# Writing the even pairs' score banks from VectorE in each image's last attention block

## The reference

```
h = group_norm1(x, n2_g, n2_b)
N = H * W
q = conv1x1(h, q_w, q_b).reshape(B, C, N).transpose(0, 2, 1)
k = conv1x1(h, k_w, k_b).reshape(B, C, N)
v = conv1x1(h, v_w, v_b).reshape(B, C, N).transpose(0, 2, 1)
scale = C ** (-0.5)
attn = jax.nn.softmax(jnp.einsum('bnc,bcm->bnm', q, k) * scale, axis=-1)
out = jnp.einsum('bnm,bmc->bnc', attn, v)
return x + out
```

## Time and profile before

| | us |
|---|---|
| median of 3 runs | 2844.68 (2842.29 to 2845.42) |
| profiled execution, its own time | 2840.18 |
| profiled execution, its span | 2838.4 |

### The profile page before, as it was taken

One profiled execution on the slowest core, in us unless ns is written; L12 is line 12 of the kernel. 1 busy time (PEld: TensorE's weight loads), 2 busy tenths in 40 slices (PEclk: granted clock), 3 DMA queues, 4 the chain that ended last, 5 costly groups with the idle time before them and its releaser, 6 DMA issues.

```text
span 2838.4 us, 54486 instructions
## 1 busy us (share of the span) xinstructions
PE 2763.5 (97%) x19644; PEld 933.7 (33%) x19644; DVE 2519.0 (89%) x3182; ACT 2223.6 (78%) x2321; POOL 1826.2 (64%) x1479
## 2 busy tenths in 40 slices
PE   7889999999999999999988999999999999999998
PEld 4233333333333333333323333333333333333332
DVE  5689999999999999999768999999999999999984
ACT  4467888888888888888866788888888888888887
POOL 1446666666666666666664666666666666666666
PEclk9999999999999999999999999999999999999999
DMA  6103000000000000000000000000000000000000
GB/s 203 40 9 75 10 11 10 11 10 10 11 10 11 11 10 11 10 11 9 5 5 16 9 10 11 10 11 10 11 10 11 11 10 11 11 10 11 9 5 5
DMA packets 35768, 48.20 MB, mean 17 GB/s; under 512 B 7848, under 2 KB 33960, under 8 KB 34992
## 3 DMA queue, kind: packets, MB, share of 16 engines
q1 hardware_dynamic: 35504, 44.75, 6.0%
HBM read 16.41 MB, written 9.44 MB: 9 GB/s over the span
## 4 chain that ended last, share of the span: by engine, by line
PE 88%; DVE 8%; issue 3%; ACT 1%; POOL 0%; DMA 0%; POOLq 0%; DVEq 0%; SPq 0%; ACTq 0%
PE ps L950 39%; PE ps L941 33%; PE ps L957 11%; DVE mxp L759 4%; PE ps L1058 2%; DVE arena L782 1%; DVE ps L772 1%; PE ps L973 1%; ACT arena L532 0%; DVE ps L775 0%; PE ps L1085 0%; PE ps L1034 0%; PE ps L1142 0%; PE ps L1100 0%; PE ps L966 0%
## 5 line engine op out<-in xcount | busy, mean ns | idle before, releaser
L462 POOL TENSOR_TENSOR arena<-arena 128x512 f32<-128x512 f32 x1224 | 1559.6, 1274 | 798.0 <-ACT arena L532 719.1
L759 DVE TENSOR_REDUCE mxp<-ps 128x1 f32<-128x1024 f32 x1296 | 1575.3, 1219 | 169.0 <-PE ps L957 137.8
L532 ACT ACTIVATE arena<-ps,bnd 128x1024 f32<-128x1024 f32 x1296 | 1374.0, 1111 | 412.8 <-PE ps L941 368.7
L950 PE MATMUL ps<-arena,vals 128*64 128x512 f32 x5184 | 1268.2, 605 | 1.0 <-ACT pvb L542 1.0
L941 PE MATMUL ps<-arena 64*128 64x512 f16 x7776 | 1054.9, 377 | 4.7 <-ACT ps L569 2.9
L775 DVE TENSOR_TENSOR ps<-ps,arena 128x512 f32<-128x512 f32 x1260 | 869.0, 690 | 72.1 <-ACT arena L532 71.2
L569 ACT ACTIVATE ps<-mseed 128x1024 f32<-128x1024 f32 x612 | 629.2, 1028 | 53.3 <-ACT arena L532 0.4
L957 PE MATMUL ps<-arena,QM 64*128 64x512 f16 x2592 | 500.9, 383 | 17.8 <-DVE mxp L759 11.0
L941 PEld LDWEIGHTS ps<-arena 64*128 64x128 f16 x7776 | 375.2, 94 | 423.4 <-issue 31.0
L950 PEld LDWEIGHTS ps<-arena,vals 128*64 128x64 f32 x5184 | 310.8, 136 | 505.4 <-issue 349.1
L957 PEld LDWEIGHTS ps<-arena,QM 64*128 64x128 f16 x2592 | 124.7, 93 | 734.9 <-DVE mxp L759 633.3
(11 more groups left out here) (111 smaller groups left out, 674.4 us busy)
## 6 DMA issues: line engine op xcount, KB each, us to landing
arena<-arena SPq DMA_DIRECT2D x144, 64.0 KB, 2.0
arena<-in_x_rows SPq DMA_DIRECT2D x8, 816.0 KB, 10.0
xs<-in_x SPq DMA_DIRECT2D x4, 1152.0 KB, 16.3
f_scratch<-arena SPq DMA_DIRECT2D x32, 144.0 KB
f<-f_scratch SPq DMA_DIRECT2D x16, 288.0 KB, 9.7
QM<-arena SPq DMA_DIRECT2D x72, 64.0 KB, 2.0
xst<-arena SPq DMA_DIRECT2D x72, 64.0 KB, 1.9
out<-ot SPq DMA_DIRECT2D x72, 64.0 KB, 2.0
```

The costliest lines, as they stand in the source:

```text
L462: nc.gpsimd.tensor_tensor(accA[:, n % 2, :], accA[:, n % 2, :], e, ALU.add).then_inc(adda_free, 1)
L532: nc.scalar.activation(flat(E[:, slot_of(n % 2, p), :, :]), flat(ps[:, S_BANK + 2 * buf:S_BANK + 2 * buf + 2, :]), ACT.Exp, scale=bnd[:, 6 ...
L759: nc.vector.reduce_max(flat(mxp[:])[:, v:v + 1], flat(ps[:, bank:bank + 2, :]), AX.X).then_inc(mx_free, 1)
L950: a = nc.tensor.matmul(ps[C * t:C * t + C, ACC_BANK, :], V[:, p, t, :], E[:, slot_of(par, p), t, :], start=(p == 0), stop=(p == NPAIR - 1) ...
```

## The change

In the last block of an image (`j == NBLK - 1`) VectorE writes `mseed` over the banks of the even pairs 4 to 34, except pair 10, whose bank 0 is used in between for the row sums of the block before: 15 pairs per image, 30 in all. The scores of these pairs leave out their fourth term (two matmuls) and wait for the new semaphore `dve_filled`.

```diff
+        def dve_fills(j, p):
+            return j == NBLK - 1 and 4 <= p < NPAIR and p % 2 == 0 and p != ROW_SUMS + 4
+
+        FILLS = sum(dve_fills(NBLK - 1, p) for p in range(NPAIR))
...
+            def fill(b, j, p):
+
+                n = blk(b, j)
+                dve.wait_ge(mseed_ready, n + 1)
+                dve.wait_ge(e_ready, NPAIR * n + p)
+                nc.vector.tensor_copy(ps[:, S_BANK:S_BANK + 2, :], mseed[:, n % 2, :].unsqueeze(1).to_broadcast([P, 2, CH])
+                                      ).then_inc(dve_filled, 1)
...
@@ def attend(b, j) on VectorE, inside the loop over p @@
+                    if dve_fills(j, p + 2):
+                        fill(b, j, p + 2)
                     if p + 1 < NPAIR:
                         add_b(n, p + 1)
...
-            def scores(par, p, peers, seeds=None):
+            def scores(par, p, peers, seeds=None, fills=None):
...
-                if seeds is not None:
-                    pe.wait_ge(seeded, seeds)
+                if seeds is not None or fills is not None:
+                    if seeds is not None:
+                        pe.wait_ge(seeded, seeds)
+                    else:
+                        pe.wait_ge(dve_filled, fills)
                     terms = terms[:3]
...
-                                             start=(k == 0 and seeds is None), stop=(k == len(terms) - 1),
+                                             start=(k == 0 and seeds is None and fills is None), stop=(k == len(terms) - 1),
...
-                        scores(par, p + 2, n0 + p + 1)
+                        fills = FILLS * b + sum(dve_fills(j, q) for q in range(p + 3)) if dve_fills(j, p + 2) else None
+                        scores(par, p + 2, n0 + p + 1, fills=fills)
```

More of the change, by code:

```diff
@@ L223, in program @@
         seeded = sem("seeded")
+        dve_filled = sem("dve_filled")
         s_ready = sem("s_ready")
```

## The result

The kernel with the change takes 2861.52 us (median of 4 runs, 2859.27 to 2863.14), the kernel before 2844.84 (4 runs): slower, ratio 1.0061, 95% interval 1.0049 to 1.0074. The forecast was 2860.8. The profiled execution took 2859.27 us, with a span of 2857.5, so it is 19.1 us above the profiled execution before; the medians are 16.7 us apart. The profiled execution before was itself a quick one, 4.5 us under its kernel's median; where the rest of the difference lies is told further down.

What follows compares the result with a forecast made beforehand. TensorE bounds the last block, ScalarE close behind; a chain through VectorE makes turns 3.93 us against 3.54, or 4.23 with a reciprocal. That adds 8.04 us per image, 16.1 in all: 2844.68 + 16.1 = 2860.8 us, range 2854 to 2867.

Steps and rivals of the forecast that it cites:

- Signal to TensorE: Chain link in an image's last block: end of VectorE's instruction to the waiting matmul, 0.07 us.
- ScalarE's 0.16: High end for the signal link: from ScalarE's seed end to the waiting matmul, 0.16 us.
- The reciprocal: Stands between add and copy in eight turns per image: 0.30 us more, a turn of 4.23 us.
- +0.75: Last block, pair 2 to 4: 3.18 us now, 3.93 with the change.
- +0.47: Last block, pairs 4 to 8, two turns: 7.39 us now, 7.86 with the change.
- -0.22: Last block, pair 8 to 10: no copy, TensorE bounds it with one fourth term less, 0.22 us saved.
- +0.45: Last block, pair 10 to 12: 3.48 us now, 3.93 with the change.
- +5.49: Last block, pairs 12 to 28, eight turns with a reciprocal: 28.35 us now, 33.84 with the change.
- +1.10: Last block, pairs 28 to 34, three turns: 10.69 us now, 11.79 with the change.
- rival 2: Last blocks: copy hidden in the 1.42 us slack, 6.6 us saved, 2838.1 us; chance 4%.
- Double rate for the copy: Rival 1, VectorE's copy in last blocks: 0.82 us for 1024 columns, +3.8 us, 2848.5 us; chance 7%.
- A lower clock: Rival 3, last blocks: TensorE's clock halves in the chain's gaps, +96 us, some 2940 us; chance 1%.

Runs made afterwards that it cites:

- run 1: Changed kernel with VectorE's copy for pair p + 2 placed ahead of its add of pair p, and so ahead of the reciprocal: 2841.24 us, ratio 0.9993.
- run 2: Changed kernel with the last block's eight reciprocals moved behind the odd pair's add, none between add and copy: 2858.43 us, ratio 1.0048.
- run 5: Changed kernel with copies of 512 columns instead of 1024 (bank 0 only), bank 1's tile keeping its fourth term: 2851.56 us, ratio 1.0028.
- run 3: Changed kernel with copies made and waited for, but the even pairs' scores keep their fourth term and start=True: 2868.88 us, ratio 1.0089.
- run 8: Kernel before, last blocks' odd seeds from pair 5 cut in two (ScalarE bank 2, VectorE bank 3), no copies for even pairs: 2841.63 us, ratio 0.9991.
- run 7: Run 1 plus last blocks' odd seeds from pair 5 cut in two (ScalarE bank 2, VectorE bank 3): 2840.99 us, ratio 0.9989.
- run 4: Changed kernel without copies or their waits, 30 scores with three terms, output not the reference's: 2839.97 us, ratio 0.9988.
- run 6: Changed kernel with the even pairs' copies made by ScalarE behind its even exponentials instead of by VectorE: 2867.26 us, ratio 1.0082.
- run 9: Run 8 with run 4's edit: odd seeds cut in two, three terms in 30 scores, no copies, output not the reference's: 2836.32 us, ratio 0.9974.
- run 10: Run 7 with VectorE's copies only for every second even pair, the others keeping four terms: 2841.04 us, ratio 0.9992.

## Why the prediction was right

**The mechanism.** The forecast was the chain exponentials, add, copy, six matmuls, with both TensorE and ScalarE waiting for it. The chain in the trace is that one, link by link, and four runs take its links apart: without the add and the reciprocal ahead of the copy the loss is gone (run 1), without the reciprocal it falls by 0.25 us a turn (run 2), with a copy 0.53 shorter and scores 0.22 longer it falls by 0.31 (run 5), with two more matmuls it grows by 0.22 (run 3).

**The links.** Exponentials to add: 1.15 forecast, 1.15 measured. Add to copy 0.61 and 0.61. Copy 1.23 and 1.21 to 1.22. Signal to TensorE 0.07 and 0.14: the row chosen was the wrong one. The prediction's other figure, ScalarE's 0.16, is nearer but was no signal either: the odd pair's matmuls at 1417.33 come 0.22 after the two ahead of them, as they do without any wait. Where they do wait for the seed, it is 0.14 (shown below). Six matmuls 0.87 and 0.86. Sum 3.93 and 3.98. The reciprocal 0.30 and 0.25, so the turn with one was met (4.23 and 4.23) by two errors of opposite sign.

**The sum.** Per image, in the prediction's order, forecast and measured: +0.75 and +0.80; +0.47 and +0.57; -0.22 and -0.12; +0.45 and +0.50; +5.49 and +5.48; +1.10 and +1.25. Together +8.04 and +8.48, so 17.0 us for both images where 16.1 were forecast and the medians show 16.7. The -0.12 is pair 8 to 10: the exponentials come 0.86 us after the scores' start at pair 8 (six matmuls) but 1.08 at pair 10 (eight), which takes back the 0.22 of the term, and what is left is the 0.1 us for which the odd pair no longer waits for its seed. The mechanism was right; that the forecast of 2860.8 came within 0.7 us of the median is in part luck, since the links were 0.9 us too short in all and single executions of the kernel before lie up to 3 or 4 us from their median.

**What was imprecise.** "TensorE bounds the block, and ScalarE comes close behind" was not quite so. The prediction saw the wait for the seed, but put it into the turn that it showed, where there is none. It stands in every other turn, as in these rows of both engines, before:

```profile
1419.75 1.03 ACT L569 ACTIVATE ps<-mseed 128x1024 f32<-128x1024 f32 x1
...
1420.60 0.38 PE L941 MATMUL ps<-arena,one 64*128 64x512 f16 x2
...
1420.92 0.82 PE L941 MATMUL ps<-arena 64*128 64x512 f16 x6
```

The seed ends at 1420.78, and the matmuls start 0.14 later, 0.32 after the two ahead of them instead of 0.22. So what ran at 3.54 us was a loop over two turns and both engines: exponentials to the end of the seed and its signal 3.38, scores of the odd pair 0.75, weighing 1.87, scores of the even pair 1.08, together 7.08 (the recorded expectations have 3.40 and 7.10). All turns are down to TensorE's own 3.48 only when the seed comes earlier (run 8). For the forecast it made no difference, as its chain is longer than both. But the price of rival 2, 6.6 us for a hidden copy, was too high: the loop contains the even pair's scores once in two turns, so the removed terms bring half. Measured are 3.9 us for the terms alone (3.0 by the turns of its trace) and 2.7 us with the copy first (run 1, median against median, an interval that includes no change).

**The rivals.** Double rate for the copy: 30 copies took 1206 to 1220 ns, single rate, as the 512-column row had said. The Trainium skill, "VectorE: DVE Perf Modes", has it in another section, "Why PSUM operands drop a tier": an operand in PSUM caps a float32 instruction at single rate. The trace agrees, also for an instruction whose output alone lies there. A hidden copy: its condition, add and copy and signal in 1.42 us, did not hold; they took 2.0. The order of run 1, without the add ahead, needs 1.48 and so comes close. No run made the copy so short or so early that it was hidden with room to spare. A lower clock: it did not come, the granted clock was 1.00 in every 5 us window of both last blocks from pair 2 on.

**What the forecast did not see.** The profiled execution after is 2.1 us longer than two blocks explain. From the first image's end (ScalarE's copy of the weighed values) to ScalarE's first use of the second image's maxima it is 79.88 us before and 81.53 after, although the instructions there are the same: 1.65 of the 2.1 us. The last section has what is known of it.

**A version that beats both.** Run 7, 2840.99 us against 2843.79, is 0.1% faster than the kernel before, with an interval that just excludes 1; run 1 is the smallest edit that undoes the loss. Nothing tells the two apart. With the chain through the copy at 3.45 and TensorE's own work at 3.27, about 0.18 us a turn remain that no run which keeps the maximum in every pair reached.

## What to carry to other kernels

An engine that is idle for half of a stage is still not a free place for work: count from the event that starts the work to the one that needs it, through everything that stands ahead of it in that engine's order. Here 0.61 us of add and 0.25 of reciprocal ahead of a copy decided between a loss of 17 us and none. And when a link is taken off the busiest engine, look for loops that span two iterations and two engines before pricing the gain by that engine's work.

## What the runs showed of the hardware

Between the images the instructions are the same in all these kernels, but the granted clock is not the same in their traces. Windows before, then after, from the same event (about 3 us past ScalarE's first copy of weighed values, and about 33 us past it):

```profile
1460.00:1465.00 5.00, 2.64 (x6) 1.08 (x7) 4.68 (x11) 3.32 (x5) 2.83 (x3) 1.00 0.01 2
...
1490.00:1495.00 5.00, 4.20 (x8) 1.51 (x6) 0.38 (x3) 3.92 (x6) 0.00 (x0) 0.79 0.10 26
```

```profile
1468.00:1473.00 5.00, 2.52 (x5) 1.13 (x4) 4.33 (x11) 3.32 (x5) 2.48 (x2) 0.75 0.00 0
...
1498.00:1503.00 5.00, 4.55 (x6) 1.97 (x7) 1.54 (x7) 2.57 (x5) 0.75 (x1) 0.50 0.00 0
```

With nearly the same work, the clock is 1.00 in the one and 0.75 in the other (part of the stretch at 1.2 instead of 2.4 GHz), and later 0.79 and 0.50; the same eight matmuls of a projection (L1142, now L1163) span 5.28 us in the one and 6.73 in the other. In the six traces of the kernels before, after and runs 1 to 4 the stage takes 79.9 us twice (before, run 4) and 81.1 to 81.6 us four times. The other traces have 81.2 to 81.6 (runs 5 to 9) and 80.3 (run 10). The two quick ones are the two kernels in which no engine makes an additional or divided copy, so the traces alone, one for each kernel, cannot clear the copies. The medians speak rather against them. In runs 1, 5, 7, 8 and 9, each with such copies and at least 8 runs, the distance from the kernel before is what the turns of the last blocks give, to within 0.5 us, with no 1.2 to 1.7 us on top; but each of these medians has an interval of some 2.5 us either way, and runs 2 and 3, with 4 runs each, do lie 1.6 us above their turns. So chance in the profiled executions before and of run 4 is the likelier reason; the cause, and what decides when the clock falls and rises, stay open. It is a spread of 1.7 us in a stage that none of these kernels changes, as large as some of the effects measured here.

Two matmuls of 64 rows that work on the two halves of the partitions took as long as one: each further two of 512 columns took 0.22 us, and when only one of the two was left, nothing was saved (run 5: scores of seven matmuls start at 1426.32 and the weighing at 1427.93, 1.61 us later; in run 3, with eight, they start at 1428.04 and 1429.65, also 1.61).
